# Cross-attention in a one-core fp32 decoder: the first head's softmax tiles turned through DRAM and VectorE, and scaled on ScalarE

## The chip, the cores and the metric

One core of a Trainium2 chip runs the whole program in one launch. The time is that of the program on the device, in microseconds; the median of three runs of the kernel before is 3028.91 us (3027.8 to 3032.17).

## What is computed

The reference is one decoder layer over 16 sequences of 512 tokens of width 512, all in float32: a linear attention block with a short convolution, a masked multi-query cross-attention, and a gated recurrent feed-forward block that runs along the batch axis. Only the second is touched here. With `xn` and `mn` the normalised tokens and memory, it is:

```python
q = jnp.einsum('BTD,NDH->BTNH', xn, q_w)            # 4 heads of 128
kv = jnp.einsum('BSD,cKDH->cBSKH', mn, kv_w)        # one key head, one value head
q = _apply_rope(q, q_pos) * HEAD_DIM ** (-0.5)
k = _apply_rope(k, k_pos)
logits = jnp.einsum('BTKGH,BSKH->BKGTS', q, k)
masked = jnp.where(mem_mask[:, None, None, None, :], logits, MASK_FILL)
probs = jax.nn.softmax(masked, axis=-1)
enc = jnp.einsum('BKGTS,BSKH->BTKGH', probs, v)
return jnp.einsum('BTNH,NHD->BTD', enc, out_w)
```

The order in which the 512 keys of a sequence stand in the rows of `probs` is free, as long as values and mask follow it.

## The kernel before

The program has four phases that follow each other on every engine: a (linear attention), b (cross-attention), c (the recurrent gates) and d (the output). Every float32 product is three TensorE products of rounded halves (`product`: high by high, high by low, low by high), so each operand of a product is split: ScalarE writes the high half, and VectorE or GpSimd the rest, "low".

**Phase b** is a software pipeline (`pipeline3`) over the 16 sequences. Step s works on up to three of them: `new` = s, `old` = s - 1 and `fin` = s - 2. Within a step each engine walks the same loop `for j in range(J)` with J = 16, four heads by four tiles of 128 queries; this text calls one pass of it a slot. The engines are in-order queues that meet through semaphores, so the order of the lines inside a slot is the order in which an engine must do them.

What happens to tile j of `old`:

- TensorE computes its logits two slots ahead (`logits`, slot j - 2), into one of two banks; it waits until the bank's last tile has been masked (`top_sb`).
- VectorE masks them and takes the row maximum (`masked`, line 1531, also slot j - 2), writing one of four slots of the tile `soft`. It first waits until that slot is free: before the change, until TensorE has turned the tile four back.
- ScalarE takes the exponential (`exp`, line 1379, slot j - 2). VectorE takes one over the sum (`one_over`, line 1520) and GpSimd multiplies by it (`normalise`, line 1316), both in slot j - 1.
- TensorE turns the tile by four 128x128 transposes (`turn_p`, line 1723, at the end of slot j) into one of two banks `b_t`.
- In slot j + 1 ScalarE writes the high half (`p_high`, line 1388) and VectorE the low half (`p_low`, line 1539).
- TensorE multiplies head h by the values (`encode`): head 0 in slot 8, head 1 in slot 11, head 2 in slots 13 to 15, and head 3 in slot 1 of the next step.

Around it, in the same step: the keys and values of `new` (slots 0 to 3, `keys` on VectorE in 3 and 4), the output projection of `fin` (TensorE slots 4 to 7, `residual` on VectorE in slots 5 to 8), the turn of the new keys (slot 7), and the queries of `new` (slots 9 on). The tokens `x` of `new` reach the queries so: ScalarE normalises tiles 0 and 1 in slot 15 and tiles 2 and 3 in slot 0 (line 1158); SyncE stores x to the DRAM tensor `out` (line 1118), waits for it and loads it back with its 128x128 blocks exchanged (`load_shuffled`, line 382, four DMAs); VectorE transposes the 32x32 squares (`tokens_turned`, line 388, one chunk in each of slots 5 to 8); ScalarE makes the high half in the same slots (`tokens_high`, line 1416, ahead of that slot's `exp`) and GpSimd the low half in slots 6 to 8 (line 1320). ScalarE splits the memory of the next sequence in slots 6 to 9 (`memory_high`, line 1243), at the end of each slot.

SyncE issues all DMAs, in this order in a step: `res` of `fin` (line 1279), the x store and the four x loads of `new`, then for the next sequence the mask (line 1127), the memory (line 1109, after `kv_ps` says that the old one has been read) and x (line 1114), and the store of `fin`'s result (line 1302).

The program's own functions that the diff touches are printed here, with the line numbers of the profile:

Of the kernel before, what the change touches and what calls it, by code (L numbers as in the profile page):

```python
# [12 lines left out]
P = 128  # L13
# [183 lines left out]
class Kernel:  # L197
# [842 lines left out]
    def phase_b(self, ctx):  # L1040
# [5 lines left out]
        SLOTS = 4  # L1046
        with ExitStack() as held:
# [8 lines left out]
            q = self.split(ctx, "b_q", [P, H, S])  # L1056
            p = [self.split(ctx, f"b_p{i}", [P, T, S]) for i in range(2)]
            memT = Split(sb("memT_hi", [P, C, S], F32R), Place(nc, self.base + 1024 * 196).tile("b_memT_lo", [P, C, S], F32R))
# [33 lines left out]
            kv_ps, v_hi, v_lo = ev("kv_ps", 2), ev("v_hi", 2 * T), ev("v_lo", T)  # L1092
            k_rope = ev("k_rope", 8)
            kT_ps, k_hi, k_lo = ev("kT_ps"), ev("k_hi"), ev("k_lo")
            x_moved = ev("x_moved", 5, 16)
            x_turned, xT_hi, xT_lo = ev("x_turned", C), ev("xT_hi", C), ev("xT_lo", C)
            q_ps, q_cos, q_swapped, q_sin, q_rope = ev("q_ps", H), ev("q_cos", H), ev("q_swapped", 2 * H), ev("q_sin", H), ev("q_rope", H)
            q_hi, q_lo = ev("q_hi", H), ev("q_lo", H)
            mask_in, mask_f = ev("mask_in", 1, 16), ev("mask_f")
            logit_ps, top_sb, p_exp, sum_one, p_norm = ev("logit_ps", J), ev("top_sb", J), ev("p_exp", J), ev("sum_one", J), ev("p_norm", J)  # L1100
            pT_ps, p_hi, p_lo = ev("pT_ps", J), ev("p_hi", J), ev("p_lo", J)
# [4 lines left out]
            def load_mem(sp, b):  # L1106
                if b >= 1:
                    sp.wait_ge(kv_ps.sem, kv_ps.upto(b - 1))
                sp.dma_start(memT_f[:, :, :], self.token_rows(self.x2, b)).then_inc(mem_in.sem, mem_in.unit)
# [6 lines left out]
            def shuffle_x(sp, b):  # L1116
                sp.wait_ge(N.normed.sem, N.normed.upto(b))
                sp.dma_start(self.token_rows(self.out, b), x[:, :, :]).then_inc(x_moved.sem, x_moved.unit)
                sp.wait_ge(x_moved.sem, x_moved.upto(b - 1, 0))
                self.load_shuffled(sp, x, self.out, b, x_moved)  # L1120

            def load_mask(sp, b):
                if b >= 1:
                    sp.wait_ge(mask_in.sem, mask_in.upto(b - 1))
                if b >= 2:
                    sp.wait_ge(mask_f.sem, mask_f.upto(b - 2))
# [107 lines left out]
            jobs += [(k_lo, 0, 0)] + [(q_cos, h, 0) for h in range(H)]  # L1234
# [36 lines left out]

            def sync(sp):
                def step(s, new, old, fin):
                    if fin:
# [13 lines left out]
                    if s == B - 1:  # L1288
                        self.c_parameters(sp)
                        sp.wait_ge(kv_ps.sem, kv_ps.upto(B - 1))  # L1290
# [30 lines left out]

# [1178 lines left out]
```

## Time and profile before

| | |
|---|---|
| median of 3 runs | 3028.91 us |
| the profiled execution, its own time | 3028.35 us |
| its span, first to last instruction | 3026.6 us |
| busy: TensorE, VectorE, ScalarE, GpSimd | 2983.4, 1952.0, 1295.3, 919.5 us |
| granted TensorE clock, mean | 0.997 of full |
| one step of phase b | 57.2 us |

The profile has one record for each instruction of each engine, and for each DMA the time from its issue to its landing. Weight loads of TensorE overlap its matmuls. A busy share near 1 means that the engine never stood idle between modelled records.

### The profile page before, as it was taken

The numbers are of one execution on the slowest core, as the hardware profiler recorded it, in microseconds if no ns is written. First come the engines' busy times: TensorE is split into PE (matmuls) and PEld (weight loads), VectorE is DVE, ScalarE is ACT, GpSimd is POOL, SyncE is SP. The second block draws the span as 40 slices with busy tenths as digits, with TensorE's granted clock in tenths as the row PEclk, the third lists the DMA queues.
The fourth block names the chain that finished last, engine by engine and source line by source line (L and its number), as shares of the span: only waits on it lengthen the run. The fifth ranks groups of instructions, "written<-read, shape, count | busy, mean of one in ns | idle before, by whom it ended". The sixth has DMA issues, their size and how long they took to land.

```text
span 3026.6 us, 39400 instructions
## 1 busy us (share of the span) xinstructions
PE 2983.4 (99%) x14628; PEld 2508.4 (83%) x14628; DVE 1952.0 (64%) x4095; ACT 1295.3 (43%) x2511; POOL 919.5 (30%) x681
## 2 busy tenths in 40 slices
PE   7999999999989999999999999999999999999999
PEld 6888888888868888888888878888888888888887
DVE  6888888888878888888888774323333433232455
ACT  4444444444457766767766643211112212112243
POOL 0101010101357877777777720000000000000144
PEclk9999999999999999999999999999999999999999
DMA  7777777777733334344344232111111121111486
GB/s 212 201 203 209 202 215 199 215 198 217 205 105 113 105 107 127 99 113 127 99 114 126 71 125 74 56 54 55 42 42 42 56 55 57 42 28 46 153 290 224
DMA packets 319631, 380.07 MB, mean 126 GB/s; under 512 B 15312, under 2 KB 175056, under 8 KB 319440
## 3 DMA queue, kind: packets, MB, share of 16 engines
q1 hardware_dynamic: 319440, 377.56, 43.2%
q8 instruction: 116, 1.90, 0.3%
q14 instruction: 75, 0.61, 0.1%
HBM read 232.80 MB, written 130.02 MB: 120 GB/s over the span
## 4 chain that ended last, share of the span: by engine, by line
PE 96%; DVE 2%; ACT 1%; issue 1%; DMA 0%; POOL 0%; SPq 0%; DVEq 0%; ACTq 0%; POOLq 0%
PE c_p L132 11%; PE c_p L131 11%; PE c_p L130 11%; PE a_p L130 6%; PE a_p L131 6%; PE a_p L132 6%; PE b_n L130 5%; PE b_n L132 5%; PE b_n L131 5%; PE b_t L1723 3%; PE d_p L131 2%; PE d_p L132 2%; PE d_p L130 2%; PE a_p L1017 2%; PE a_r L131 2%; PE a_r L132 2%
## 5 line engine op out<-in xcount | busy, mean ns | idle before, releaser
L1316 POOL TENSOR_SCALAR b_soft<-b_soft,b_one_in_sum 128x512 f32<-128x512 f32 x256 | 401.2, 1568 | 201.5 <-DVE b_one_in_sum L1520 201.3
L1997 ACT ACTIVATE c_gate<-c_p,c_bias 128x512 f32<-128x512 f32 x180 | 124.2, 690 | 682.6 <-PE c_p L132 682.6
L2027 DVE TENSOR_TENSOR c_gate<-c_gate,c_gate 128x512 f32<-128x512 f32 x64 | 44.2, 691 | 502.7 <-ACT c_gate L1997 502.7
L351 POOL TENSOR_TENSOR kept_scale<-c_ln_ve,minus_half 128x4 f32<-128x4 f32 x16 | 16.1, 1008 | 880.4 <-DVE c_ln_ve L343 880.4
L1531 DVE CUSTOM_DVE_ANT_0 b_soft<-b_l,b_mask_row 128x512 f32<-128x512 f32 x256 | 175.6, 686 | 87.9 <-issue 84.0
L351 POOL TENSOR_TENSOR a_ln_sc<-a_ln_ve,minus_half 128x4 f32<-128x4 f32 x16 | 16.3, 1017 | 629.9 <-DVE a_ln_ve L343 629.9
L1379 ACT ACTIVATE b_soft<-b_soft,b_minus_top 128x512 f32<-128x512 f32 x256 | 184.5, 721 | 44.6 <-DVE b_minus_top L1531 42.6
L649 ACT ACTIVATE a_elu<-a_p 128x512 f32<-128x512 f32 x128 | 75.6, 591 | 287.6 <-PE a_p L132 287.6
L1388 ACT ACTIVATE b_p_hi<-b_t 128x512 fp32r<-128x512 f32 x256 | 151.3, 591 | 109.9 <-PE b_t L1723 109.6
L1539 DVE TENSOR_TENSOR b_p_lo<-b_t,b_p_hi 128x512 fp32r<-128x512 f32 x256 | 175.7, 686 | 16.1 <-ACT b_p_hi L1388 14.3
L1723 PE MATMUL b_t<-ident,b_soft 128*128 128x128 f32 x1024 | 154.5, 273 | 4.9 <-POOL b_soft L1316 4.9
L2221 POOL TENSOR_TENSOR d_x<-d_x,d_y 128x512 f32<-128x512 f32 x60 | 79.8, 1332 | 252.8 <-ACT d_y L2238 252.8
L1723 PEld LDWEIGHTS b_t<-ident,b_soft 128*128 128x128 f32 x1024 | 126.0, 142 | 30.5 <-DVE b_p_lo L1539 6.4
L130 PE MATMUL b_l<-b_k_hi,b_q_hi 128*128 128x512 f32 x256 | 123.2, 481 | 2.0 <-POOL b_q_lo L1328 1.6
L2029 DVE TENSOR_TENSOR c_gate<-c_gate,c_c_f 128x512 f32<-128x512 f32 x64 | 44.3, 692 | 116.3 <-ACT c_gate L1997 116.3
L130 PE MATMUL a_p<-a_Wk_hi,a_xT_hi 128*128 128x512 f32 x256 | 105.3, 411 | 0.7 <-DVE a_Wk_lo L194 0.7
L626 POOL TENSOR_TENSOR a_res<-a_res,a_bp 128x512 f32<-128x512 f32 x64 | 82.3, 1318 | 75.9 <-DMA a_res<-in_x 47.4
L666 ACT ACTIVATE a_z_hi<-a_z_sum 128x512 fp32r<-128x512 f32 x64 | 40.5, 633 | 150.2 <-DVE a_z_sum L848 150.2
L130 PE MATMUL b_n<-b_nT_hi,b_qw_hi 128*128 128x512 f32 x256 | 100.7, 393 | 3.0 <-POOL b_nT_lo L1320 3.0
L130 PE MATMUL b_e<-b_p_hi,b_v_hi 128*128 128x512 f32 x256 | 100.4, 392 | 2.9 <-DVE b_enc_lo L1544 2.9
L132 PE MATMUL b_l<-b_k_hi,b_q_lo 128*128 128x512 f32 x256 | 102.0, 398 | 0.0
L130 PE MATMUL a_r<-a_Wp_hi,a_z_hi 128*128 128x512 f32 x256 | 101.2, 395 | 0.0
(301 smaller groups left out, 9617.6 us busy)
## 6 DMA issues: line engine op xcount, KB each, us to landing
a_mem_moving<-in_ctx SPq DMA_DIRECT2D x64, 256.0 KB, 5.2
a_mem_turned<-in_ctx SPq DMA_DIRECT2D x16, 1024.0 KB, 9.2
x<-a_mem_turned SPq DMA_DIRECT2D x16, 1024.0 KB, 7.8
a_res<-in_x SPq DMA_DIRECT2D x16, 1024.0 KB, 6.4
x<-a_res SPq DMA_DIRECT2D x16, 1024.0 KB, 5.2
b_memT_f<-x SPq DMA_DIRECT2D x16, 1024.0 KB, 7.3
b_x<-x SPq DMA_DIRECT2D x16, 1024.0 KB, 6.1
b_res<-x SPq DMA_DIRECT2D x16, 1024.0 KB, 5.5
```

The source lines that it names most:

```text
L130: pe.matmul(out, stationary.high, moving.high, start=first, stop=False)
L131: pe.matmul(out, stationary.high, moving.low, start=False, stop=False)
L132: return pe.matmul(out, stationary.low, moving.high, start=False, stop=last)
L626: pool.tensor_tensor(res[:, t, :], res[:, t, :], bp[:, :], ALU.add).then_inc(res_bp.sem, res_bp.unit)
L1316: pool.tensor_scalar(soft[:, at, :], soft[:, at, :], one_in_sum[:, at:at + 1], None, ALU.mult).then_inc(p_norm.sem, p_norm.unit)
L1379: act.activation(soft[:, at, :], soft[:, at, :], ACT.Exp, bias=minus_top[:, at:at + 1], scale=-1.0, accum_out=row_sum[:, at:at + 1]).then_ ...
L1388: act.activation(p[h % 2].high[:, :, t * P:(t + 1) * P], pT_banks[j % 2][:, :].rearrange("p (i s) -> p i s", i=T), ACT.Copy).then_inc(p_hi ...
L1531: dve.tensor_tensor_reduce(out=soft[:, at, :], in0=logit_banks[j % 2][:, :], in1=mask_row[b % 2][:, :], scale=-1.0, scalar=3e38, op0=ALU.a ...
L1539: dve.tensor_tensor(part.low, pT_banks[j % 2][:, :].rearrange("p (i s) -> p i s", i=T), part.high_f32(), ALU.subtract).then_inc(p_lo.sem, ...
L1723: mm = pe.transpose(pT_banks[j % 2][:, i * P:(i + 1) * P], soft[:, tile(old.b, j), i * P:(i + 1) * P], self.ident[:, :])
L1997: act.activation(gate[j % 2][i][:, :], gating.banks[(3 * j + i) % 6][:, :], ACT.Tanh if g == "c" else ACT.Sigmoid, bias=added[:, i, j:j + ...
L2221: pool.tensor_tensor(x[old.par][:, t, :], x[old.par][:, t, :], y[:, t % 2, :], ALU.add).then_inc(out_sb.sem, out_sb.unit)
```

## The change

For the first head (tiles 0 to 3 of each sequence) the four TensorE transposes of each tile are gone. ScalarE, no longer GpSimd, multiplies the tile by one over the sum. SyncE stores it to rows of `out` (256 KB), waits for that, and loads it back with its 128x128 blocks exchanged by four DMAs of 64 KB into the one buffer `p_shuffled`; VectorE transposes the 32x32 squares into `p0_raw` (the place of `p[0].low`); ScalarE makes the high half, and GpSimd the low half in place. All keys, the mask and the transposes of the other 12 tiles go over to an interleaved order of the keys (key i*128 + w at column 4*w + i). Several semaphores are merged (`kvq_ps`, `k_mask`), which changes no order.

The new parts, cut to their core:

```diff
+            def shuffle_p(sp, b, t):
+                rows = self.out[b, t * P:(t + 1) * P, :]
+                sp.wait_ge(p0_norm.sem, p0_norm.upto(b, t))
+                sp.dma_start(rows, soft[:, t, :]).then_inc(p_moved.sem, p_moved.unit)
+                sp.wait_ge(p_moved.sem, p_moved.upto(b, 5 * t))
+                if b >= 1 or t >= 1:
+                    sp.wait_ge(p_lo.sem, p_lo.upto(b - (t == 0), first_turned_at[t - 1]))
+                for a in range(4):
+                    sp.dma_start(p_shuffled[32 * a:32 * (a + 1), 0, :]..., rows[:, a * P:(a + 1) * P]...).then_inc(p_moved.sem, p_moved.unit)
+            def soft_free(b, j):
+                g = b * J + j - SLOTS
+                if g < 0:
+                    return None
+                item, k = divmod(g, J)
+                if k < T:
+                    return p_moved.sem, p_moved.upto(item, 5 * k)
+                return pT_ps.sem, pT_ps.upto(item, k - T)
 # SyncE, per step
+                    if old:
+                        shuffle_p(sp, old.b, 0)
+                    if new and new.b >= 1:
+                        store_x(sp, new.b)
+                    if old:
+                        shuffle_p(sp, old.b, 1)
                     if new and new.b >= 1:
                         shuffle_x(sp, new.b)
+                    if old:
+                        shuffle_p(sp, old.b, 2)
+                        shuffle_p(sp, old.b, 3)
                     if following(new, B):
                         load_mask(sp, new.b + 1)
                         load_mem(sp, new.b + 1)
                         load_x(sp, new.b + 1)
 # GpSimd
-                        if old and j < J - 1:
+                        if old and T <= j + 1 < J:
                             normalise(old.b, j + 1)
-                        if new and j == J - 1:
-                            normalise(new.b, 0)
+                        if old and HEAD <= j < HEAD + T:
+                            first_head_low(j - HEAD)
 # ScalarE, first in the slot
-                        if old and j >= 1:
+                        if old and j < T - 1:
+                            first_head_normalise(old.b, j + 1)
+                        if new and j == J - 1:
+                            first_head_normalise(new.b, 0)
+                        if old and j >= T + 1:
                             p_high(old.b, j - 1)
+                        if old and HEAD <= j < HEAD + T:
+                            first_head_high(j - HEAD)
 # VectorE, masked(b, j)
-                        if free := earlier(pT_ps, b, j, SLOTS):
+                        if free := soft_free(b, j):
                             dve.wait_ge(*free)
 # VectorE, after masked(old.b, j + 2) and ahead of tokens_turned(j - 5)
-                        if old and j >= 1:
+                        if old and j >= T + 1:
                             p_low(old.b, j - 1)
+                        if old and HEAD - 1 <= j < HEAD - 1 + T:
+                            first_head_turned(j - HEAD + 1)
+                    def first_head_turned(t):
+                        dve.wait_ge(p_moved.sem, p_moved.upto(old.b, 5 * t + 4))
+                        ...
+                        dve.transpose(p0_raw[:, :, t * P:(t + 1) * P], blocks).then_inc(p_lo.sem, p_lo.unit)
 # TensorE
-                        if old:
+                        if old and j >= T:
                             turn_p(j)
-                            mm = pe.transpose(..., soft[:, tile(old.b, j), i * P:(i + 1) * P], self.ident[:, :])
+                            mm = pe.transpose(..., interleaved(soft[:, tile(old.b, j), :], i, T), self.ident[:, :])
 # TensorE, encode
+                            if h == 0:
+                                pe.wait_ge(p0_lo.sem, p0_lo.upto(item.b))
```

HEAD is 4 and T is 4; `first_turned_at` makes the loads of tile t wait until VectorE has turned tile t - 1 out of `p_shuffled`. The x store and the wait for it now stand on either side of the second tile's five DMAs.

## Rows read from the trace of the kernel before

**Rows 1.** Page: busy, chain by engine; one step by windows (PE, PEld, DVE, ACT, POOL, clock, DMA).

```profile
PE 2983.4 (99%) x14628; PEld 2508.4 (83%) x14628; DVE 1952.0 (64%) x4095; ACT 1295.3 (43%) x2511; POOL 919.5 (30%) x681
...
PE 96%; DVE 2%; ACT 1%; issue 1%; DMA 0%; POOL 0%; SPq 0%; DVEq 0%; ACTq 0%; POOLq 0%
...
1335.67:1392.89 57.22, 57.22 (x310) 48.64 (x309) 47.47 (x128) 39.90 (x86) 44.51 (x33) 1.00 0.39 112
```

**Rows 2.** Timeline of TensorE: a tile's four transposes, contiguous and interleaved, with the next product.

```profile
1393.76 0.60 PE L1723 MATMUL b_t<-ident,b_soft 128*128 128x128 f32 x4
1394.11 0.48 PE L130 MATMUL b_l<-b_k_hi,b_q_hi 128*128 128x512 f32 x1
1394.43 0.39 PE L131 MATMUL b_l<-b_k_lo,b_q_hi 128*128 128x512 f32 x1
...
851.20 0.64 PE L369 MATMUL b_n<-ident,b_x 128*128 128x128 f32 x4
851.59 0.48 PE L130 MATMUL a_r<-a_Wp_hi,a_z_hi 128*128 128x512 f32 x1
```

**Rows 3.** Timeline of the DMA queue in one step (start, time on the queue, line, tensors).

```profile
1337.99 0.38 SPq L1118 DMA_DIRECT2D out<-b_x  x1
1342.31 1.93 SPq L382 DMA_DIRECT2D b_x<-out  x4
1344.34 0.43 SPq L1127 DMA_DIRECT2D b_mask_u<-in_mask_BxS_bk  x1
1345.72 0.38 SPq L1109 DMA_DIRECT2D b_memT_f<-x  x1
...
1395.22 0.38 SPq L1118 DMA_DIRECT2D out<-b_x  x1
```

**Rows 4.** DMA issues: count, KB each, median us to landing; the last row is one issue's, the fourth x load.

```profile
out<-b_x SPq DMA_DIRECT2D x1, 1024.0 KB, 4.3
b_memT_f<-x SPq DMA_DIRECT2D x1, 1024.0 KB, 7.0
b_mask_u<-in_mask_BxS_bk SPq DMA_DIRECT2D x1, 64.0 KB, 5.8
out<-d_x SPq DMA_DIRECT2D x4, 256.0 KB, 2.0
c_x_shuffled<-c_x SPq DMA_DIRECT2D x16, 64.0 KB, 2.1
DMA to landing us min/median/max: 6.2/6.2/6.2
```

**Rows 5.** Timeline of VectorE, same step: masked tiles 5 and 6, and the first x transpose.

```profile
1344.32 0.69 DVE L1531 CUSTOM_DVE_ANT_0 b_soft<-b_l,b_mask_row 128x512 f32<-128x512 f32 x1 [0.61 <-issue]
...
1347.77 0.69 DVE L1531 CUSTOM_DVE_ANT_0 b_soft<-b_l,b_mask_row 128x512 f32<-128x512 f32 x1
...
1351.99 1.08 DVE L388 STREAM_TRANSPOSE b_nT_f<-b_x 128x512 f32<-128x512 f32 x1
```

**Rows 6.** Groups by line: one operation's mean ns on ScalarE, VectorE and GpSimd.

```profile
L1158 ACT ACTIVATE b_x<-b_x,b_n_bias,b_n_scale 128x512 f32<-128x512 f32 x60 | 45.6, 809 | 0.3
L1416 ACT ACTIVATE b_nT_hi<-b_nT_f 128x512 fp32r<-128x512 f32 x60 | 38.0, 633 | 122.7 <-DVE b_nT_f L388 122.7
L1320 POOL TENSOR_TENSOR b_nT_lo<-b_nT_f,b_nT_hi 128x512 fp32r<-128x512 f32 x60 | 77.8, 1297 | 5.6 <-ACT b_nT_hi L1416 5.6
```

**Rows 7.** Timeline, same step: logits 8 on TensorE, ScalarE's first memory half, the first head's product.

```profile
1353.65 0.47 PE L130 MATMUL b_l<-b_k_hi,b_q_hi 128*128 128x512 f32 x1
...
1358.21 0.62 ACT L1243 ACTIVATE b_memT_hi<-b_memT_f 128x512 fp32r<-128x512 f32 x1
...
1362.60 0.40 PE L130 MATMUL b_e<-b_p_hi,b_v_hi 128*128 128x512 f32 x1
```

**Rows 8.** TensorE at the start of phase b: two waits, then the granted clock by windows.

```profile
907.50 0.50 PE L130 MATMUL b_n<-b_nT_hi,b_qw_hi 128*128 128x512 f32 x1 [2.37 <-POOL b_nT_lo L1320]
...
909.00:912.40 3.40, 3.24 (x10) 0.50 0.90 340
```

More of the change, by code:

```diff
@@ L1046, in phase_b @@
         SLOTS = 4
+        HEAD = 4
         with ExitStack() as held:
@@ L1056, in phase_b @@
             q = self.split(ctx, "b_q", [P, H, S])
+            p0_at = self.place.offset
             p = [self.split(ctx, f"b_p{i}", [P, T, S]) for i in range(2)]
+            p0_raw = Place(nc, p0_at + 4 * T * S).tile("b_p0_raw", [P, T, S])
+            p_shuffled = Place(nc, self.d_bo_at).tile("b_p_shuffled", [P, 1, S])
             memT = Split(sb("memT_hi", [P, C, S], F32R), Place(nc, self.base + 1024 * 196).tile("b_memT_lo", [P, C, S], F32R))
@@ L1233, in phase_b @@
             jobs = [(k_rope, 2, 0), (k_rope, 6, 0)] + [(x2_sb, t, 2) for t in range(T)]
-            jobs += [(k_lo, 0, 0)] + [(q_cos, h, 0) for h in range(H)]
+            jobs += [(k_mask, 0, 0)] + [(q_cos, h, 0) for h in range(H)]
             pT_banks = self.banks(held, "b_t", 2)
@@ L1389, in p_high, with first_head_normalise, first_head_high @@
                                        ACT.Copy).then_inc(p_hi.sem, p_hi.unit)
+                    def first_head_normalise(b, t):
+                        act.wait_ge(sum_one.sem, sum_one.upto(b, t))
+                        at = tile(b, t)
+                        act.activation(soft[:, at, :], soft[:, at, :], ACT.Copy, scale=one_in_sum[:, at:at + 1]).then_inc(p0_norm.sem, p0_norm.unit)
+                    def first_head_high(t):
+                        act.wait_ge(p_lo.sem, p_lo.upto(old.b, first_turned_at[t]))
+                        part = (slice(None), slice(None), slice(t * P, (t + 1) * P))
+                        act.activation(p[0].high[part], p0_raw[part], ACT.Copy).then_inc(p_hi.sem, p_hi.unit)
                     def enc_high(b, h):
@@ L1585, in keys_low @@
                         dve.wait_ge(k_hi.sem, k_hi.upto(new.b))
-                        dve.tensor_tensor(k[new.par].low[:, :], turns.bank(s, KT)[:, :], k[new.par][:, :].high_f32(), ALU.subtract).then_inc(k_lo.sem, k_lo.unit)
+                        dve.tensor_tensor(by_column(k[new.par].low), by_tile(turns.bank(s, KT)), by_column(k[new.par].high.bitcast(F32)), ALU.subtract).then_inc(k_mask.sem, k_mask.unit)
                     def mask():
@@ L1718, in turn_p @@
                     def turn_p(j):
-                        if free := earlier(p_lo, old.b, j, 2):
-                            pe.wait_ge(*free)
-                        pe.wait_ge(p_norm.sem, p_norm.upto(old.b, j))
+                        if j >= T + 2:
+                            pe.wait_ge(p_lo.sem, p_lo.upto(old.b, low_at[j - 2]))
+                        elif old.b >= 1:
+                            pe.wait_ge(p_lo.sem, p_lo.upto(old.b - 1, low_at[J - 2 - T + j]))
+                        pe.wait_ge(p_norm.sem, p_norm.upto(old.b, j - T))
                         for i in range(T):
-                            mm = pe.transpose(pT_banks[j % 2][:, i * P:(i + 1) * P], soft[:, tile(old.b, j), i * P:(i + 1) * P], self.ident[:, :])
+                            mm = pe.transpose(pT_banks[j % 2][:, i * P:(i + 1) * P], interleaved(soft[:, tile(old.b, j), :], i, T), self.ident[:, :])
                         mm.then_inc(pT_ps.sem, pT_ps.unit)
```

72 lines of the change are left out of this document (46 added, 26 removed).

## The prediction

> **What bounds the kernel now.** The page comes first: TensorE is busy for 2983.4 of 3026.6 us and makes up 96% of the chain that ended last [rows 1]. The windows show one step of phase b fully covered: 57.22 us, all PE, at full granted clock, with VectorE busy for 47.5, ScalarE for 39.9, GpSimd for 44.5 and the DMA engines for 0.39 [rows 1]. Successive x stores are 57.23 us apart [rows 3], so the step repeats at TensorE's pace. Two questions follow: what the change takes from TensorE, and whether what it puts on the other queues still arrives in time. The second needs the DMA queue and the order inside the slots, and the rest of the working is a walk through one step, in the trace's own times.
>
> **What TensorE saves.** A tile's four transposes start at 1393.76 and the next product at 1394.11, which is 0.35 us; that product's successor starts 0.32 later instead of 0.23, so 0.09 more [rows 2]. That gives 0.44 us a tile, 1.8 a step, and 28 us over 64 tiles: 3000 if all of it shows. The other 12 tiles are now read interleaved. Such a group took 0.39 against 0.35 [rows 2], so 0.04 each: 0.5 us a step. The merged semaphores and the key order on ScalarE and VectorE change no count and no size; I cost them at nothing, covered by the idle time that both engines have in a step [rows 1], and at 0.1 us a step if that cover is gone.
>
> **What ScalarE, GpSimd and VectorE get.** ScalarE gains four multiplications of 128x512, between 0.63 (a copy) and 0.81 (scale and bias) us each [rows 6]; I take 0.7. Two of them stand ahead of the x normalisation in slots 15 and 0, where ScalarE has no idle time, so the x store moves from 1337.99 to about 1339.4. They also push the high and low halves of `fin`'s third head ahead of TensorE's product in slot 1: at most 1.4 us a step, less some 0.8 of slack, so 0.6. GpSimd swaps four multiplications for four subtractions of 1.30 [rows 6] and does not gain work. VectorE swaps four `p_low` for four square transposes of 1.09 [rows 5], 0.4 more each; two of the four now stand in slots 5 and 6 ahead of the x transposes. VectorE's idle 9.7 us a step [rows 1] could cover that by itself. The DMA queue is another matter.
>
> **How the queue orders things.** The mask's 64 KB, issued at 1344.34 right behind the x loads, took 5.8 us [rows 3, 4], against 2.1 for 64 KB elsewhere [rows 4]: a DMA waits behind the earlier ones. The x loads leave in 1.93 us, and the fourth lands 6.2 us after its own issue, so all are in 5.7 us after the last is issued. The memory's 1 MB landed at 1345.72 + 7.0 = 1352.7, 2.6 after the mask, so 256 KB queued behind something adds 0.65 [rows 3, 4].
>
> The Trainium skill agrees: DMA: Bandwidth & Descriptors, section "Queues, rings and completion order", says that descriptors are consumed in ring order and that a semaphore's increment lands only after the engine's earlier writes. The trace agrees with it through the mask's 5.8 us.
>
> **The walk.** Tile 0 is scaled by 1331.4, stored (2.0) and loaded (0.48 an issue, 2.1 to land) by 1337.5: early. The x store goes at 1339.4 and lands 4.3 later, tile 1's store 0.65 behind it at 1344.4; `masked(5)` ran at 1344.32 [rows 5], so it is just in time.
>
> 1. VectorE turns tile 0 in slot 3, 1345.0 to 1346.1. Only then may SyncE load tile 1 (four issues, to 1348.1), then x (to 1350.0, landed 1355.7), and then store tile 2: landed 1356.4.
> 2. `masked(6)` in slot 4 writes into the slot of `soft` that tile 2 must have left. It ran at 1347.77 [rows 5] and now waits until 1356.4. Its result is due for TensorE's logits of slot 6 at 1353.65 [rows 7], earlier by the saving. So TensorE stands here already: the store of tile 2 is queued behind 1 MB of x, and behind the VectorE pass that frees `p_shuffled`.
> 3. Turning tile 1 follows `masked(6)` in VectorE's order: done at 1358.2. SyncE then loads tile 2 (to 1360.1) and stores tile 3: landed 1362.3, and `masked(7)` ends at 1363.0. The low half of tile 4 (0.6), the turn of tile 2 (1.0) and the first x transpose (1.0) end at 1365.7; before, at 1353.07 [rows 5]: 12.6 late.
> 4. ScalarE's high half of x (0.6) and `exp` (0.8), VectorE's `one_over`, `masked(8)`, low half of tile 5 and turn of tile 3 bring us to 1369.6. Its loads, issued from 1364.6, landed at 1368.2.
> 5. SyncE issues the memory load only after tile 3's loads, at 1367.1; with 7.0 to land [rows 4] it is there at 1374.1. ScalarE's first memory half, at 1358.21 before [rows 7], waits for it with the high halves of tiles 6 and 3 behind it. Tile 3's is done at 1375.7 and GpSimd's low half (1.30) at 1377.0.
> 6. TensorE's product of the first head, at 1362.60 before [rows 7], starts at 1377.1: **14.5 us late**. The x tokens arrive just ahead of the queries, so nothing is added there. In slots 9 to 15 TensorE is the bound again, and the other engines catch up.
>
> The saving of slots 0 to 3 is swallowed by the wait, and so are the 0.6 of slot 1. Fourteen steps have x and memory to load: 14 x 14.5 = 203. Step 15 has no memory load: 12.4. Step 16 has no x either: about 1. Interleaved reading shows in slots 8 to 15 alone: 8 x 0.04 x 15 = 5. Together 221 us.
>
> **The clock.** The trace of before shows waits like these once: after 2.37 us of standing still [rows 8] and a shorter wait, TensorE's clock was granted at 0.50, its lower level of 1.2 GHz, for 3.4 us, which costs half of that, 1.7 us [rows 8]. The walk has four waits of 2 to 4.5 us in a row, the last one ending where TensorE becomes the bound. I add one such stretch a step: 15 x 1.7 = 26 us. Its bounds are 0 and two stretches, 51.
>
> The Trainium skill, TensorE: Matmul & The Clock Gate, section "HAM oscillation — how this bites in real kernels", describes a loop whose every pass waits on a DMA and starts again at the lower clock. By it the 26 us would stand in full or more; without it the sum would be 3249. Before the change only the start of phase b bears on it [rows 8].
>
> **Sum.** 3028.35 + 221 + 26 = 3275 us, made against the profiled execution, whose own time is 0.6 us below the median of the three runs.
>
> **Rivals.**
> - *Short waits.* Same mechanism, but tile 2's store does not stand behind the x loads and lands 2.0 us after its issue. Then `masked(6)` starts at 1352.0, 4.4 earlier, all that follows goes about as much earlier, and the product is 10 late: 3028 + 15 x 10 = 3178, without a stretch at the lower clock. Against it: the mask's 5.8 us.
> - *Long waits.* Two stretches at the lower clock, and every load 1 us slower through contention (three of them in the chain): 17.5 + 3.4 a step, 3340.
> - *The DMAs are hidden, and it is faster.* TensorE's saving shows in full if tile 2's store lands before about 1351, so that logits 8 are on time, and each later item stays within its slack. It brings 1.3 us a step, what is left after interleaved reading: 3028 - 16 x 1.3 = 3007. For it: the DMA engines are idle for 0.61 of a step, VectorE for 9.7 us and ScalarE for 17. Against it: the tile must pass SyncE behind nine DMAs and a VectorE pass that is itself in slot 3. It decides where that store lands 5 us earlier than the walk says.
> - *Only ScalarE's move costs.* As the last, with 0.6 us lost in slot 1 and more in the x chain: within 6 us of before.
>
> **Chances.** Forecast 0.62, short waits 0.2, long waits 0.1, hidden 0.06, only ScalarE 0.02. The range 3140 to 3330 takes in the short waits with 38 us below them, and the upper clock bound; it leaves out the faster cases and most of the long. A difference of 0.2%, 6 us, is about what a measurement of this kernel can tell. Faster 0.05, same 0.03, slower 0.92.
>
> **What would show it.** After the change a step should be near 73 us; TensorE should wait in slots 6 to 8 for `b_minus_top` (logits), `b_p_lo` or `b_res`, and for GpSimd's low half of tile 3, some 16 us in all; VectorE's `masked` should wait 8 to 9 us for the store of tile 2 in slot 4 and about 2 in slot 5; ScalarE's first memory half should wait for its DMA by about 2; the granted clock should read below 1 in phase b. Steps of under 59 us, or a tile 2 store that lands with the x loads still under way, would make the prediction wrong. A step of 73 us with the waits elsewhere would make its reasons wrong.

## The result and the profile after

The kernel after the change takes **3289.69 us** (median of four runs, 3284.76 to 3293.45), the kernel before 3029.58 on the same chip (3027.8 to 3032.17, four runs): a ratio of 1.0855, with an interval of 1.0842 to 1.0868. That is 260 us slower; the forecast was 3275, range 3140 to 3330. The profiled execution took 3284.76 us, its span 3283.0.

The page after the change: busy time by engine, the clock row of its second part, and the chain that ended last.

```profile
span 3283.0 us, 39271 instructions
...
PE 3055.0 (93%) x14372; PEld 2540.2 (77%) x14372; DVE 1953.3 (59%) x4095; ACT 1333.0 (41%) x2575; POOL 912.8 (28%) x681
...
PEclk9999999999988999999898999999999999999999
...
PE 65%; DVE 10%; DMA 9%; ACT 6%; issue 5%; SPq 3%; POOL 0%; DVEq 0%; ACTq 0%; POOLq 0%
```

Against [rows 1], TensorE runs 256 matmuls fewer and is yet busy for 71.6 us more: the part of phase b in which it runs at its lower clock stretches it. Its share of the chain falls from 96% to 65%; VectorE, DMA and ScalarE now carry a quarter.

Where the time came from is told by three rows of ScalarE's timeline, its normalisation of x tile 0 for the first, the eighth and the last of the 15 sequences for which it is done at this place.

```profile
877.84 0.80 ACT L1179 ACTIVATE b_x<-b_x,b_n_bias,b_n_scale 128x512 f32<-128x512 f32 x1
...
1390.61 0.80 ACT L1179 ACTIVATE b_x<-b_x,b_n_bias,b_n_scale 128x512 f32<-128x512 f32 x1
...
1907.48 0.80 ACT L1179 ACTIVATE b_x<-b_x,b_n_bias,b_n_scale 128x512 f32<-128x512 f32 x1
```

Before, the first and the last stood at 877.73 and 1676.68; the row that is set beside the inner one further on, at 1333.36, is the ninth, and inner steps of the kernel before repeat to 0.01 us. So nothing is lost ahead of phase b, fourteen steps lose 230.7 us (16.5 each in the mean: 73.5 us a step for 57.1), and the other 25.6 are lost in the two last steps: the product of the last head in the last step waits for `b_enc_lo` until 1779.94 before and 2036.27 after, 256.3 later, and from there to the end the two kernels take the same time.

**The DMA queue of one step** answers to [rows 3]; the columns are start, time on the queue, line and tensors.

```profile
1395.84 0.40 SPq L1137 DMA_DIRECT2D out<-b_x  x1
1396.28 0.51 SPq L1127 DMA_DIRECT2D out<-b_soft  x1
1403.13 1.76 SPq L1132 DMA_DIRECT2D b_p_shuffled<-out  x4
1404.93 2.03 SPq L382 DMA_DIRECT2D b_x<-out  x4
1407.00 0.74 SPq L1127 DMA_DIRECT2D out<-b_soft  x1
1415.00 1.74 SPq L1132 DMA_DIRECT2D b_p_shuffled<-out  x4
1416.78 0.43 SPq L1127 DMA_DIRECT2D out<-b_soft  x1
...
1423.72 0.43 SPq L1117 DMA_DIRECT2D b_memT_f<-x  x1
```

The store of tile 2 leaves at 1407.00, right behind the x loads, and by the DMA view of that stretch it takes 6.0 us to land. VectorE's `masked(6)` stands behind it, then `masked(7)` behind the store of tile 3. VectorE's timeline, with `masked`'s first instruction and the wait ahead of it:

```profile
1413.16 0.06 DVE L1597 MEMSET b_carrier<- 128x1 f32 x1 [8.35 <-DMA out<-b_soft]
...
1419.03 0.06 DVE L1597 MEMSET b_carrier<- 128x1 f32 x1 [2.35 <-DMA out<-b_soft]
...
1421.31 1.04 DVE L388 STREAM_TRANSPOSE b_nT_f<-b_x 128x512 f32<-128x512 f32 x1
```

TensorE's timeline, the waits of the same step; the last is the first head's product of [rows 7]:

```profile
1413.95 0.80 PE L130 MATMUL b_l<-b_k_hi,b_q_hi 128*128 128x512 f32 x1 [4.29 <-DVE b_minus_top L1598]
...
1427.81 0.66 PE L1861 MATMUL b_n<-ident,b_k_f 128*128 128x128 f32 x4 [1.78 <-DVE b_res L1624]
...
1433.09 0.47 PE L130 MATMUL b_e<-b_p_hi,b_v_hi 128*128 128x512 f32 x1 [3.44 <-POOL b_p_lo L1371]
```

And by windows, the whole step, from its first tile's store to the next step's, the part with the waits, and the part behind them (columns as in [rows 1]):

```profile
1388.17:1460.53 72.36, 61.51 (x293) 50.55 (x292) 47.18 (x127) 42.13 (x90) 44.20 (x33) 0.93 0.39 118
1405.00:1437.00 32.00, 21.15 (x81) 15.93 (x80) 17.16 (x40) 9.51 (x21) 16.20 (x12) 0.84 0.41 105
1437.00:1460.00 23.00, 23.00 (x115) 19.45 (x114) 18.38 (x53) 16.74 (x35) 19.99 (x15) 0.99 0.41 137
```

TensorE is idle for 10.85 us and busy for 61.5 with 293 matmuls, where before it was busy for 57.22 with 310 [rows 1]. Part of what the walk counted as waiting is therefore work at half speed. It comes in two stretches: from 1413.9 to 1420.2, behind the wait of 4.29 us, the granted clock is 0.50, between 1420.2 and 1433.8 it is 1.00, and from 1433.8 to 1437.3, behind the wait of 3.44 us, 0.51. This step is one of the milder ones: it is 15.1 us late where the mean of the fourteen is 16.5, and over those fourteen TensorE is idle for 12.5 us a step and the mean clock is 0.90. The waits over the whole run (total, times, longest):

```profile
DVE b_carrier L1597 <- DMA out<-b_soft: 183.6, 47, 9.5
...
PE b_l L130 <- DVE b_minus_top L1598: 70.6, 19, 6.3
...
PE b_e L130 <- POOL b_p_lo L1371: 59.7, 16, 4.8
...
PE b_n L1861 <- DVE b_res L1624: 26.8, 14, 2.8
...
ACT b_memT_hi L1264 <- DMA b_memT_f<-x: 26.4, 14, 3.0
```

### The profile page after: what moved, and what is told of

It is laid out like the page before. It is cut to its first block, busy times and chain, and to the rows that moved or that the text cites. A ratio compares the mean times of both kernels' runs of the same rounds, so it can differ in the third digit from the quotient of the medians.

```text
span 3283.0 us, 39271 instructions
## 1 busy us (share of the span) xinstructions
PE 3055.0 (93%) x14372; PEld 2540.2 (77%) x14372; DVE 1953.3 (59%) x4095; ACT 1333.0 (41%) x2575; POOL 912.8 (28%) x681
## 4 chain that ended last, share of the span: by engine, by line
PE 65%; DVE 10%; DMA 9%; ACT 6%; issue 5%; SPq 3%; POOL 0%; DVEq 0%; ACTq 0%; POOLq 0%
PE c_p L132 10%; PE c_p L130 10%; PE c_p L131 10%; DMA out<-b_soft 6%; PE a_p L130 5%; PE a_p L132 5%; PE a_p L131 5%; DMA b_memT_f<-x 3%; SPq L1132 2%; DVE b_p_lo L1606 2%; PE d_p L132 2%; PE d_p L131 2%; PE d_p L130 2%; PE a_p L1017 2%; PE a_r L131 2%
## 5 line engine op out<-in xcount | busy, mean ns | idle before, releaser
L1362 POOL TENSOR_SCALAR b_soft<-b_soft,b_one_in_sum 128x512 f32<-128x512 f32 x192 | 300.7, 1566 | 342.3 <-DVE b_one_in_sum L1587 342.2
L130 PE MATMUL b_l<-b_k_hi,b_q_hi 128*128 128x512 f32 x256 | 123.4, 482 | 72.2 <-DVE b_minus_top L1598 70.6
L130 PE MATMUL b_e<-b_p_hi,b_v_hi 128*128 128x512 f32 x256 | 116.4, 455 | 64.3 <-POOL b_p_lo L1371 59.7
L1606 DVE TENSOR_TENSOR b_p_lo<-b_t,b_p_hi 128x512 fp32r<-128x512 f32 x192 | 131.9, 687 | 53.0 <-ACT b_p_hi L1439 51.2
L1801 PEld LDWEIGHTS b_t<-ident,b_soft 128*128 128x128 f32 x768 | 122.7, 206 | 32.5 <-DVE b_p_lo L1606 13.2
L1439 ACT ACTIVATE b_p_hi<-b_t 128x512 fp32r<-128x512 f32 x192 | 112.6, 586 | 78.6 <-PE b_t L1801 78.0
L1801 PE MATMUL b_t<-ident,b_soft 128*128 128x128 f32 x768 | 126.3, 288 | 14.6 <-DVE b_p_lo L1606 8.3
L130 PE MATMUL b_n<-b_ow_hi,b_enc_hi 128*128 128x512 f32 x256 | 115.8, 453 | 19.1 <-DVE b_res L1624 10.0
L1597 DVE MEMSET b_carrier<- 128x1 f32 x256 | 15.1, 59 | 183.6 <-DMA out<-b_soft 183.6
L130 PEld LDWEIGHTS b_e<-b_p_hi,b_v_hi 128*128 128x128 f32 x256 | 55.1, 215 | 89.0 <-issue 67.2
L1477 ACT ACTIVATE b_nT_hi<-b_nT_f 128x512 fp32r<-128x512 f32 x60 | 37.8, 631 | 186.7 <-DVE b_nT_f L388 186.7
L130 PEld LDWEIGHTS b_l<-b_k_hi,b_q_hi 128*128 128x128 f32 x256 | 52.9, 207 | 77.6 <-DVE b_minus_top L1598 75.0
L131 PE MATMUL b_e<-b_p_lo,b_v_hi 128*128 128x512 f32 x256 | 111.9, 437 | 0.0
```

The lines of the kernel that those rows point to most:

```text
L130: pe.matmul(out, stationary.high, moving.high, start=first, stop=False)
L131: pe.matmul(out, stationary.high, moving.low, start=False, stop=False)
L1362: pool.tensor_scalar(soft[:, at, :], soft[:, at, :], one_in_sum[:, at:at + 1], None, ALU.mult).then_inc(p_norm.sem, p_norm.unit)
L1439: act.activation(p[h % 2].high[:, :, t * P:(t + 1) * P], pT_banks[j % 2][:, :].rearrange("p (i s) -> p i s", i=T), ACT.Copy).then_inc(p_hi ...
L1606: dve.tensor_tensor(part.low, pT_banks[j % 2][:, :].rearrange("p (i s) -> p i s", i=T), part.high_f32(), ALU.subtract).then_inc(p_lo.sem, ...
L1801: mm = pe.transpose(pT_banks[j % 2][:, i * P:(i + 1) * P], interleaved(soft[:, tile(old.b, j), :], i, T), self.ident[:, :])
```

## The experiments

The theory for them: the loss is the queue. Tile 2's store stands on SyncE behind the loads of tile 1 (which wait for VectorE's turn out of the one buffer `p_shuffled`) and behind 1 MB of x, so `masked`, the x transposes, the memory and the product are late in turn. Rivals: ScalarE's scaling, the interleaved reading, or the round trip itself, whatever its order. The ratios are to runs of the kernel before on the same chip, with their intervals. The experiments ran on several chips, and the kernel before took between 3029.6 and 3032.5 us on them, so a difference in us between two of the kernels is good to some 3 us. The code excerpts are cut to the lines that matter.

### The stores of tiles 1 to 3 ahead of the x loads

```diff
 # SyncE, store_p and load_p are the halves of shuffle_p
-                        shuffle_p(sp, old.b, 1)
+                        store_p(sp, old.b, 1)
+                        store_p(sp, old.b, 2)
+                        store_p(sp, old.b, 3)
+                        load_p(sp, old.b, 1)
                     if new and new.b >= 1:
                         shuffle_x(sp, new.b)
-                        shuffle_p(sp, old.b, 2)
-                        shuffle_p(sp, old.b, 3)
+                        load_p(sp, old.b, 2)
+                        load_p(sp, old.b, 3)
```

> The changed kernel with one thing moved: SyncE issues the stores of tiles 1, 2 and 3 right behind the x store, each on a count of its own, and the loads stay where they were. Theory (the store of tile 2 is late because SyncE issues it behind the turn of tile 0 and the x loads, and the soft slot is held until then): both masked waits for a store go from 9 and 2 us a step to under 1; what is left is the late turn of tiles 2 and 3 ahead of x and the memory load, about 6 us a step: 3028 + 15 x 6 = 3118, up to 3145 with stretches at the lower clock. Rival (the one buffer p_shuffled and the round trips through DRAM decide, and the masked waits only cover them): over 3230.

Measured: 3181.69 us, 1.0504 (1.0488 to 1.052), clock 0.977. 108 of the 260 us come back, and the masks' wait is gone: `b_l` waits for `b_minus_top` for 1.7 us in all, against 70.6. The theory holds for that part; 3118 to 3145 was too low, and the rival's 3230 too high. What stays is mostly the one buffer. The queue of one step:

```profile
1349.37 2.84 SPq L1148 DMA_DIRECT2D out<-b_soft  x3
1355.92 1.76 SPq L1158 DMA_DIRECT2D b_p_shuffled<-out  x4
1357.73 2.03 SPq L392 DMA_DIRECT2D b_x<-out  x4
1360.94 8.53 SPq L1158 DMA_DIRECT2D b_p_shuffled<-out  x8
```

The loads of tiles 2 and 3 take 8.53 us to issue, eight of them with a turn of VectorE between, and VectorE's turns wait for them for 73.7 us over 33 times. The product still waits for `b_p_lo` 58.5 us over 16.

### The x round trip taken away

This kernel leaves out the store and the loads of x, so that the queries are computed from other data.

```diff
-                        store_x(sp, new.b)
                         ...
-                        shuffle_x(sp, new.b)
                         ...
+                        for t in range(T):
+                            shuffle_p(sp, old.b, t)
```

> The changed kernel without the x round trip: x is neither stored to out nor loaded back with its blocks exchanged, so the queries are computed from tokens in another order (this part of the computation is changed). Theory: the store of tile 2 is issued 2 us earlier and lands 2 us after its issue in place of 6, so masked(6) starts 6 us earlier a step and all behind it: 3290 - 15 x 6 = 3200. Rival (the handover of the one buffer through VectorE decides and x only fills the time): 3280 to 3295.

Measured: 3183.54 us in one run (no interval), where 3200 was expected. The tile stores' median to landing falls from 2.7 to 2.1 us. The x traffic is thus worth some 106 us of the 260. That it costs them by standing in front of a store is shown by the kernel above, which keeps x and gains as much. And 154 us, 9.6 a step over the 16 that move tiles, remain with no x on the queue at all: VectorE's `masked` still waits 74.2 us over 31 times for a store that SyncE could not issue before the previous tile had been turned.

### ScalarE's scaling alone, in the kernel before

```diff
 # GpSimd
-                        if old and j < J - 1:
+                        if old and T <= j + 1 < J:
                             normalise(old.b, j + 1)
-                        if new and j == J - 1:
-                            normalise(new.b, 0)
 # ScalarE
+                        if old and j < T - 1:
+                            first_head_normalise(old.b, j + 1)
+                        if new and j == J - 1:
+                            first_head_normalise(new.b, 0)
```

> The kernel before with the second half of the change alone: ScalarE scales tiles 0 to 3, TensorE still turns them. Theory (the DMA chain is the cost): 3028 to 3040, at most 0.6 us a step from enc_high behind the extra work in slot 0. Rival (ScalarE's extra work in slots 15 and 0 is a good part of the loss): over 3060.

Measured: 3042.8 us, 1.0044 (1.0031 to 1.0056). A step takes some 57.9 us for 57.2. The move costs some 13 us by itself, a little above the 3028 to 3040 expected. Part of it is TensorE's wait for the late x tokens, which was 3.0 us over 2 times in the kernel before:

```profile
PE b_n L130 <- POOL b_nT_lo L1321: 7.0, 15, 2.5
```

That is 4 of the 13 us; where the rest goes wasn't followed up.

### GpSimd scales again, in the kernel after

```diff
 # GpSimd, taken from ScalarE
+                        if old and j + 1 < T:
+                            first_head_normalise(old.b, j + 1)
+                        if new and j == J - 1:
+                            first_head_normalise(new.b, 0)
```

> The changed kernel with GpSimd scaling the first head's tiles, as before the change, instead of ScalarE. Theory (the chain starts at VectorE's turn of tile 0 in slot 3, which has slack to the scaling): 3280 to 3295, within 0.3% of the changed kernel. Rival (ScalarE's share matters): under 3260, or over 3310 if GpSimd's 1.57 us delays the stores.

Measured: 3284.84 us, 1.0838 (1.0823 to 1.0853), beside 1.0855 for the change: no difference that shows. Once TensorE waits for the queue, it doesn't matter which engine scales.

### The interleaved key order alone, in the kernel before

```diff
-    ...soft[:, tile(old.b, j), i * P:(i + 1) * P], self.ident[:, :])
+    ...interleaved(soft[:, tile(old.b, j), :], i, T), self.ident[:, :])
```

with keys and mask in the same order, which ScalarE and VectorE then write and read with a stride too.

> The kernel before with the interleaved order of the keys alone: all 16 tiles of a sequence are still turned by TensorE, reading every fourth column. Theory: 0.04 us for each of 256 tiles, 3029 + 10 = 3039, and ScalarE and VectorE's strided reads of the keys hidden. Rival (weight loads of 0.21 in place of 0.14 us show fully, 4 x 0.07 x 256): 3100.

Measured: 3042.72 us, 1.0041 (1.0029 to 1.0054), a step 58.1 us. The loss is in TensorE's own time: in the profiled execution it is busy for 3000.4 us against 2983.4 and waits no longer than before, so the other engines' strided accesses don't show. What differs there is the weight loads of the transposes; the row of this kernel:

```profile
L1729 PEld LDWEIGHTS b_t<-ident,b_soft 128*128 128x128 f32 x1024 | 158.4, 206 | 19.6 <-DVE b_p_lo L1545 3.4 <-issue 2.9
```

and of the kernel before:

```profile
L1723 PEld LDWEIGHTS b_t<-ident,b_soft 128*128 128x128 f32 x1024 | 126.0, 142 | 30.5 <-DVE b_p_lo L1539 6.4 <-issue 1.0
```

Such a load takes 206 ns for 142. By the medians (3042.72 against 3031.18) the 256 tiles cost 11.5 us, 0.045 each, where the forecast took 0.04; the profiled execution, 3045.14 us, is one of the slower ones.

### The memory's loads ahead of tile 3's

```diff
-                    if following(new, B):
-                        load_mask(sp, new.b + 1)
-                        load_mem(sp, new.b + 1)
+                        shuffle_p(sp, old.b, 3, fetch)   # mask and memory between its store and its loads
```

> The changed kernel with the mask and memory loads issued between the store and the loads of tile 3, some 6 us earlier. Theory (the memory wait stands in the chain with 1.4 to 2 us a step): 3290 - 15 x 1.7 = 3264; tile 3's loads, now behind 1 MB, land near the time at which VectorE asks for them and may eat 1 us of it, so up to 3280. Rival (the memory wait is covered by the first head's other waits): 3287 to 3295.

Measured: 3318.04 us, 1.0949 (1.0934 to 1.0964): 28 us slower than the change, where 10 to 26 faster was expected. A miss. ScalarE no longer waits for the memory (26.4 us before), but tile 3's loads now stand behind the memory's 1 MB. SyncE's queue:

```profile
1435.94 0.43 SPq L1117 DMA_DIRECT2D b_memT_f<-x  x1
1436.41 2.29 SPq L1134 DMA_DIRECT2D b_p_shuffled<-out  x4
```

and two of the waits of the run:

```profile
PE b_n L1867 <- DVE b_res L1630: 89.2, 14, 8.0
...
DVE b_p_raw L1620 <- DMA b_p_shuffled<-out: 68.5, 15, 6.1
```

VectorE turns tile 3 ahead of `residual`, so all of it stands: TensorE's wait at the key turn for `b_res` rises from 26.8 to 89.2 us, while its wait for `b_p_lo` falls from 59.7 to 22.0. The sum, 25 us more, is about the loss.

### Four buffers, and two stores and loads ahead of x

The tiles land in the four chunks of `b_nT_f`, free at that time, so no load waits for a turn, and tiles 0 and 1 make their round trip before the x store.

```diff
                         store_p(sp, old.b, 0)
                         load_p(sp, old.b, 0)
+                        store_p(sp, old.b, 1)
+                        load_p(sp, old.b, 1)
                         ...
                     if new and new.b >= 1:
                         store_x(sp, new.b)
                     if old:
-                        shuffle_p(sp, old.b, 1)
+                        store_p(sp, old.b, 2)
+                        store_p(sp, old.b, 3)
                         ...
                         shuffle_x(sp, new.b)
                         ...
-                        shuffle_p(sp, old.b, 2)
-                        shuffle_p(sp, old.b, 3)
+                        load_p(sp, old.b, 2)
+                        load_p(sp, old.b, 3)
                         ...
-                    sp.dma_start(p_shuffled[32 * a:32 * (a + 1), 0, :]...
+                    sp.dma_start(nT_f[32 * a:32 * (a + 1), t, :]...
```

> The changed kernel with the DMA order rebuilt: the shuffled tiles go to four 2 KB places (the chunks of nT_f, which nobody uses from the end of the queries to the first x transpose), so no load waits for a turn; SyncE stores and loads tiles 0 and 1, then stores x, tiles 2 and 3, loads x, and loads tiles 2 and 3. ScalarE still scales. Theory (the loss is the order and the one buffer, not the number of DMAs or VectorE's work): no masked wait, no wait of the memory half, at most 1 us a step before the first x transpose; with 13 us from ScalarE's part: 3015 to 3050. Rival (VectorE's extra square transposes in slots 5 and 6 and the longer queue cost by themselves): over 3080.

Measured: 3095.84 us, 1.0215 (1.0201 to 1.0229), clock 0.988. The DMA waits are nearly gone (VectorE's turns wait 10.3 us in all), and 194 of the 260 us are back, so the queue with its one buffer was the larger cause. Order and buffer changed together here; from the kernel with the early stores, which kept the buffer, it is 86 us. But it is not the 3015 to 3050 expected. The rest is this:

```profile
PE b_e L140 <- POOL b_p_lo L1401: 33.9, 15, 3.7
PE b_n L1891 <- DVE b_res L1654: 16.0, 14, 1.8
```

VectorE's timeline, its `one_over` of successive slots, shows the pace:

```profile
1387.85 0.16 DVE L1617 RECIPROCAL b_one_in_sum<-b_row_sum 128x1 f32<-128x1 f32 x1
...
1393.11 0.16 DVE L1617 RECIPROCAL b_one_in_sum<-b_row_sum 128x1 f32<-128x1 f32 x1 [0.83 <-ACT b_soft L1460]
...
1397.94 0.16 DVE L1617 RECIPROCAL b_one_in_sum<-b_row_sum 128x1 f32<-128x1 f32 x1 [0.83 <-ACT b_soft L1460]
```

The starts are 5.26, 4.83 and (to 1402.04, behind a slot with no turn) 4.1 us apart, and the last three waited 0.83 us for ScalarE's `exp`. The reading, which the kernel after the next puts to the test: in a slot with a turn and an x transpose ScalarE's x half waits for both, `exp` stands behind the half, and the next `one_over` waits for `exp`: a loop through two engines that are both idle in part.

### Four buffers, with GpSimd scaling

The edit is the one shown above for GpSimd, on the last kernel.

> As four_buffers, and GpSimd scales the first head's tiles instead of ScalarE. Theory: 8 to 15 us below four_buffers, 3005 to 3040, as the ScalarE part alone cost 13 us over the kernel before. Rival (GpSimd's 1.57 us delays the stores of tiles 2 and 3 past the x loads): equal to four_buffers or slower.

Measured: 3134.56 us, 1.0345 (1.0331 to 1.0359): 39 us worse where a gain was expected. Two scaled tiles have to leave before x, and from GpSimd they come later: in the step looked at, the x store leaves 9.9 us behind the normalisation of x tile 0 (1390.53 to 1400.39), against 6.6 in the last kernel (1369.81 to 1376.43). VectorE's turns wait 55.2 us for their loads (10.3 before) and TensorE 32.0 for `b_res`. With the order of this queue, ScalarE is the better engine for the scaling.

### The turn last in VectorE's slot

```diff
-                        if old and HEAD - 1 <= j < HEAD - 1 + T:
-                            first_head_turned(j - HEAD + 1)
                         ...
+                        # behind tokens_turned and residual
+                        if old and HEAD - 1 <= j < HEAD - 1 + T:
+                            first_head_turned(j - HEAD + 1)
```

> four_buffers with one thing moved: in each of slots 3 to 6 VectorE turns the first head's tile as its last work of the slot, behind the x transpose and the residual, instead of ahead of them. Theory (in slots 5 to 8 VectorE and ScalarE wait for each other in turn, x transpose, tokens_high, exp, one_over, so the 1.0 us ahead of the x transpose is added to the loop in slots 5 and 6, while behind it it fills VectorE's 0.83 us wait for exp): 1.6 of the 2 us return, and the stretches at the lower clock with them: 3096 - 15 x 2 = 3066, down to 3045. Rival (VectorE's share is not the limit and GpSimd's low half in slot 7 decides): 3085 to 3100.

Measured: 3078.42 us, 1.0151 (1.0137 to 1.0165), clock 0.991, the best of all with the change in it. That is 17 us back, where 30 to 50 were expected and the rival had at most 11, so the theory of the loop holds in kind and overstated what it is worth. The starts of `one_over` are now

```profile
1437.81 0.12 DVE L1617 RECIPROCAL b_one_in_sum<-b_row_sum 128x1 f32<-128x1 f32 x1
1441.66 0.14 DVE L1617 RECIPROCAL b_one_in_sum<-b_row_sum 128x1 f32<-128x1 f32 x1
1445.57 0.14 DVE L1617 RECIPROCAL b_one_in_sum<-b_row_sum 128x1 f32<-128x1 f32 x1
```

5.16 (from 1432.65), 3.85 and 3.91 apart. A step takes some 60.1 us, with one long wait left:

```profile
1448.91 0.47 PE L140 MATMUL b_e<-b_p_hi,b_v_hi 128*128 128x512 f32 x1 [2.41 <-POOL b_p_lo L1401]
```

Tile 3 is turned too late for the product of slot 8; the wait makes up 37.6 us in all.

### The same with GpSimd scaling and x earlier

Here two things change: GpSimd scales, and SyncE stores and loads tile 0, stores x and tiles 1 to 3, loads x, then loads tiles 1 to 3.

> turned_last with GpSimd scaling the first head, and the DMA order suited to it: store and load tile 0, store x, store tiles 1 to 3, load x, load tiles 1 to 3. Theory (in four_buffers_pool the x store had slipped from 1.3 behind tile 1's scaling to 5 us late, and tile 2's loads with it): the x store leaves on time again, ScalarE's slots 15 to 2 are as before the change: 3020 to 3050, and under turned_last. Rival (GpSimd has no room for both the scaling and the low halves): over turned_last.

Measured: 3090.16 us, 1.0192 (1.0178 to 1.0206), and not the 3020 to 3050 expected. The same wait for `b_p_lo` stands (37.1 us over 15), and TensorE's `turn_p` now also waits for GpSimd's scaling, 15.0 us over 12.

### Turns and halves one slot earlier

```diff
-        HEAD = 4
+        HEAD = 3
-            first_turned_at ... = (0, 1, 3, 5), [None] * T + [2, 4] ...
+            first_turned_at ... = (0, 1, 2, 4), [None] * T + [3, 5] ...
```

> turned_last with the first head's turns, high halves and low halves one slot earlier (slots 2 to 5, 3 to 6 and 3 to 6). In turned_last the only wait of TensorE left in a step is 2.41 us for GpSimd's low half of tile 3 at the first head's product in slot 8. Theory (that wait is only a place in the order, the tiles being in SBUF in time): it goes, and the stretches at the lower clock that it brings: 3078 - 15 x (2.4 + 0.9) = 3030, between 3022 and 3045. Rival (the work moved to slots 2 to 5 is late by the same amount elsewhere, behind the loads of tiles 2 and 3 or in the loop of slots 5 and 6): 3060 to 3085.

Measured: 3092.05 us, 1.0204 (1.019 to 1.0218), above even the rival's 3060 to 3085. The rival's mechanism is what the trace shows. The wait of the product is gone from the list, but the halves, first in ScalarE's slot, now wait for the turns, and `exp` and the keys behind them:

```profile
1440.27 0.63 ACT L1480 ACTIVATE b_p_hi<-b_p_raw 128x512 fp32r<-128x512 f32 x1 [3.86 <-DVE b_p_raw L1644]
```

TensorE waits in small pieces instead: `b_nT_lo` 23.7 us over 30, `b_soft` 13.4 over 18, `b_res` 10.5 over 14.

### The same, with ScalarE's halves behind `exp`

```diff
-                        # ScalarE, first in the slot
-                        if old and HEAD <= j < HEAD + T:
-                            first_head_high(j - HEAD)
+                        # ScalarE, behind exp
+                        if old and HEAD <= j < HEAD + T:
+                            first_head_high(j - HEAD)
```

> one_slot_earlier with ScalarE's high half of the first head's tile behind that slot's exp instead of first in the slot, in slots 3 to 6. In one_slot_earlier ScalarE stands 3.9 and 2.3 us at these halves in slots 4 and 5, waiting for VectorE's turn, with the new values' high halves and exp queued behind. Theory (the loss is only in what is queued behind a wait): these waits end, the loop of values, keys and exp in slots 3 and 4 returns to its old times, and neither the first head nor the x tokens are late: 3092 - 15 x 3.5 = 3040, between 3030 and 3060, still not below the kernel before (ScalarE's scaling and the interleaved reading have cost 12 us each alone, against 28 saved). Rival (GpSimd's low halves or the loads are as late): over 3075.

Measured: 3095.96 us, 1.0214 (1.02 to 1.0228); again the rival. VectorE stands still for tile 2, whose loads are behind those of x:

```profile
1392.68 1.08 DVE L1644 STREAM_TRANSPOSE b_p_raw<-b_nT_f 128x512 f32<-128x512 f32 x1 [3.57 <-DMA b_nT_f<-out]
```

and over the whole run:

```profile
DVE b_p_raw L1644 <- DMA b_nT_f<-out: 53.8, 15, 4.5
```

**What stays open.** No version beat the kernel before. Of the 46 us by which the best one trails, 37.6 are the wait for `b_p_lo`. TensorE's saving of at most 28 is about what ScalarE's scaling and the interleaved reading cost alone, 13 and 12; that these costs add up in the changed kernel is an assumption, and the one comparison that there is (GpSimd scaling again) showed nothing. Whether an order exists that brings all four tiles and x in time wasn't found, and that none exists isn't shown. The clock's share was read from traces and not isolated by a run.

## Why the prediction was right, and where it was off

**The mechanism** stood as forecast. Shifted by 56.8 us, which puts the landing of tile 1's store on the walk's time, the rows of the step read so:

| event | walk | trace, shifted |
|---|---|---|
| store of tile 2 issued | 1350.0 | 1350.2 |
| it lands, `masked(6)` starts | 1356.4 | 1356.4 |
| store of tile 3 issued | 1360.1 | 1360.0 |
| `masked(7)` starts | 1362.3 | 1362.3 |
| first x transpose ends | 1365.7 | 1365.6 |
| memory load issued | 1367.1 | 1366.9 |
| ScalarE's first memory half | 1374.1 | 1373.2 |
| first head's product | 1377.1 | 1376.3 |

The shift is fitted at that one row; counted from ScalarE's x normalisation it would be 57.25 us, and all of the trace's times 0.45 earlier.

The bounds that decided it were those of the queue. The price of 0.65 us per 256 KB queued, worked out from [rows 3, 4], gave 6.4 us for the store of tile 2; it measured 6.0. That refutes **short waits**, whose condition was a landing in 2.0 us; the time of that rival, 3178, is about what the two kernels gave in which the stores no longer stood behind x (3182 and 3184). **Hidden** and **only ScalarE** needed the store 5 us earlier.

**Sizes that were off.**
- *The memory load* was taken at 7.0 to land and took 6.2, so the product was 13.7 us late in the walk's time and not 14.5. Counted from ScalarE's x normalisation (1333.36 and 1390.61) it is 13.2 late in this step; over the thirteen steps from the second to the fourteenth that lateness is 13.1 to 15.9 and 14.2 in the mean. The term was right for the average step.
- *TensorE's waits.* Forecast were some 16 us a step, measured 10.9 in the step shown and 12.5 in the mean. A wait that comes while the work ahead of it is at the lower clock is shorter by as much as that work is stretched.
- *The clock.* One stretch of 3.4 us a step, 1.7 lost, was added. There are two, of 6.3 and 3.5 us, together about 10 us at the lower level of 1.2 GHz, which is what the mean granted clock of 0.93 over 72.36 us says too (0.14 of the step), and 5 us more went into the same work. The first lies ahead of the product, under waits that the walk had counted already, so it adds nothing. The second starts 0.7 us behind the product's start and costs half of its 3.5 us: that is the stretch of the forecast. Behind the product the step shown loses 1.9 us (15.1 less 13.2) and the mean inner step 2.3 (16.5 less 14.2), where the forecast had 2.0 (1.7 of clock and 0.3 of interleaved reading). That one stretch was enough is in part luck: nothing in the forecast said that the other would fall under a wait.
- *The steps at the end.* This is the term of the sum that was wrong. Fourteen steps were forecast at 231 us and gave 230.7; step 15 at about 14.4, and it gave 15.9 (its wait for `b_enc_lo` ends at 1738.23 before and 1984.88 after). Step 16 was put at "about 1" because it has no x, and it lost 9.7. The timeline of that step, SyncE, VectorE and TensorE:

```profile
1996.78 1.75 SPq L1132 DMA_DIRECT2D b_p_shuffled<-out  x4
1998.57 1.23 SPq L1127 DMA_DIRECT2D out<-b_soft  x1
...
2001.94 0.06 DVE L1597 MEMSET b_carrier<- 128x1 f32 x1 [5.19 <-DMA out<-b_soft]
...
2009.22 0.75 PE L1801 MATMUL b_t<-ident,b_soft 128*128 128x128 f32 x4 [2.79 <-DVE b_p_lo L1606]
...
2018.39 0.47 PE L130 MATMUL b_e<-b_p_hi,b_v_hi 128*128 128x512 f32 x1 [1.85 <-POOL b_p_lo L1371]
```

No x load is on the queue, and still `masked(6)` waits 5.19 us, since tile 2's store can't be issued before tile 0 has been turned and tile 1's loads have left. Both waits of TensorE are new. The kernel without the x round trip says the same for every step: 9.6 us each. The walk named both causes, the x traffic and the one buffer, but priced the buffer at nothing where x was absent. The last 5 us to the median are the profiled execution's distance from it (3284.76 to 3289.69).

**The rest of the working.** VectorE's waits were forecast at 8 to 9 us and about 2; they were 8.35 and 2.35. ScalarE's wait for the memory, forecast at about 2, is 26.4 over 14, 1.9 each. ScalarE's scaling was put at 0.6 us a step in slot 1, swallowed by the wait: alone it costs 0.7 (57.9 for 57.2), though the wait that shows is for the x tokens and not in slot 1, and in the change nothing shows. TensorE's saving never showed.

The Trainium skill, TensorE: Matmul & The Clock Gate, section "HAM oscillation — how this bites in real kernels", describes a loop in which each pass starts again at the lower clock after its DMA wait. The trace agrees: the stretch of 1405 to 1437 has a granted clock of 0.84, and each of the fourteen steps between the first and the last x normalisation reads between 0.76 and 0.93, where [rows 8] had it once. The waits are for VectorE and GpSimd, behind VectorE's own wait of 8.35 us for a DMA.

## What to carry to other kernels

Before a round trip through DRAM is put on a queue that carries other transfers, walk one step of that queue with the times of the trace, and ask of each entry what stands before it and which engine's next in-order instruction waits for it: 256 KB cost 2.0 us alone and 6.0 behind 1 MB, and what waits is all that this engine has queued. Busy shares (here 0.39 for the DMA engines, 47 of 57 us for VectorE) don't answer that. Price each cause by itself in the steps that have only one of them, and remember that a single buffer turns four transfers into a chain through the engine that empties it.

## What the runs showed of the hardware that was not expected

- A stationary operand read with a stride of four fp32 elements loads in 206 ns for 142. The loads overlap matmuls, and yet the kernel with this reading alone was 11.5 us slower over 1024 of them, 0.045 us for a group of four, all of it in TensorE's busy time.
- Issuing a large transfer earlier on the same queue made the kernel slower by 28 us, since four loads of 64 KB behind 1 MB held an engine for up to 6.1 us.
- TensorE, 256 matmuls lighter, was busy for 71.6 us more: with several waits in every step, up to 4.3 us in the one shown, its granted clock was 0.93 over that step and 0.964 over the run, against 0.997 before. With one long wait of 2.4 us a step (the best variant) it was 0.991 over the run.
